# Selective-scan layers: one sequence per scan tile on four row groups of the array, and the product with C moved from VectorE to TensorE

## The reference, cut to what matters

```python
for i in range(4):                                  # N_LAYERS; D_INNER = 256, D_STATE = 16, D_CONV = 4
    u, z = split(x @ in_w[i]); u = silu(causal_conv(u, cw[i]) + cb[i])
    dt, Bm, Cm = split(u @ xpw[i])                  # 8, 16, 16 columns
    delta = softplus(dt @ dtw[i] + dtb[i])
    h[t] = exp(delta[t] * A) * h[t-1] + (delta[t] * u[t]) * Bm[t]     # h: 256 x 16 per sequence
    y[t] = sum over the 16 states n of h[t][:, n] * Cm[t][n]
    x = layer_norm((y + u * D[i]) * silu(z) @ ow[i] + x)
```

## Time and profile before

| | |
|---|---|
| median of 3 runs | 651.4 us |
| the profiled execution | 650.93 us, span 649.0 us |
| PE busy / PEld / DVE / ACT / POOL, share of the span | 85% / 65% / 72% / 48% / 26% |
| first scan of the first unit | 448.75 us |
| end of the last unit's normalisation | 630.27 us |
| TensorE clock granted, mean over the span | 0.758 of 2.4 GHz |

### The profile page before, as it was taken

One profiled execution on the slowest core, in us unless ns is written; L12 is line 12 of the kernel. 1 busy time (PEld: TensorE's weight loads), 2 busy tenths in 40 slices (PEclk: granted clock), 3 DMA queues, 4 the chain that ended last, 5 costly groups with the idle time before them and its releaser, 6 DMA issues.

```text
span 649.0 us, 20759 instructions
## 1 busy us (share of the span) xinstructions
PE 551.3 (85%) x8477; PEld 423.9 (65%) x8477; DVE 467.8 (72%) x1825; ACT 308.3 (48%) x912; POOL 168.7 (26%) x213
## 2 busy tenths in 40 slices
PE   6979877679976999999999999976898889889747
PEld 4646644468865888888888888853664666566335
DVE  2878749964446777777777777724888998899872
ACT  2778657255545443443444443434554554455401
POOL 4255725064000000000000000007437634743600
PEclk9979979899996555555555555555998998899876
DMA  8900000010011000000000000000000000000000
GB/s 317 421 17 1 3 5 1 2 47 1 1 65 36 4 4 4 5 4 5 4 4 5 4 5 4 5 1 1 1 0 2 1 1 2 0 1 2 0 0 10
DMA packets 6304, 16.07 MB, mean 25 GB/s; under 512 B 2680, under 2 KB 3488, under 8 KB 5696
## 3 DMA queue, kind: packets, MB, share of 16 engines
q1 hardware_dynamic: 5792, 14.47, 6.1%
q10 hardware_dynamic: 416, 0.26, 0.1%
HBM read 14.60 MB, written 0.13 MB: 23 GB/s over the span
## 4 chain that ended last, share of the span: by engine, by line
PE 45%; DVE 30%; ACT 13%; issue 8%; POOL 2%; DMA 1%; DVEq 0%; ACTq 0%
PE bank L1728 8%; PE bank L1634 6%; PE bank L1796 6%; ACT esp L684 3%; PE bank L1577 3%; DVE ssum L1172 2%; PE bank L1432 2%; ACT a L671 2%; ACT e L686 2%; PE bank L1422 2%; PE bank L1564 2%; DVE rz L1207 2%; DVE opre L1148 2%; DVE asp L1162 2%; DVE opre L1151 2%
## 5 line engine op out<-in xcount | busy, mean ns | idle before, releaser
L1634 PE MATMUL bank<-esp,qblk 128*128 128x1 f16 (+1 forms) x2048 | 66.6, 166 | 12.0 <-ACT esp L684 12.0
L1634 PEld LDWEIGHTS bank<-esp,qblk 128*128 128x128 f16 x2048 | 61.2, 104 | 17.3 <-ACT esp L684 17.3
L1634 PE MATMUL bank<-hsp,kT 128*128 128x2 f16 x2048 | 63.5, 166 | 2.0 <-DVE hsp L1200 1.9
L1634 PEld LDWEIGHTS bank<-hsp,kT 128*128 128x128 f16 x2048 | 59.5, 104 | 2.1 <-issue 2.1
L475 POOL MEMSET ctxT<- 128x128 f32 x1 | 0.3, 314 | 229.7 <-DVE xres L1214 229.7
L671 ACT ACTIVATE a<-opre 128x4 f32<-128x4 f32 x64 | 13.1, 205 | 80.8 <-DVE opre L1151 80.8
L1240 DVE SCALAR_TENSOR_TENSOR T<-bank,bct,T 128x256 f32<-128x256 f32 x112 | 46.4, 473 | 2.2 <-PE bank L1809 2.2
L1227 DVE TENSOR_TENSOR_SCAN qblk<-ctxT,bank 128x512 f32<-128x512 f32 x32 | 37.7, 1207 | 5.7 <-PE bank L1796 5.3
L678 ACT ACTIVATE gact<-bank,lgate 128x16 f32<-128x16 f32 x64 | 17.5, 274 | 45.7 <-PE bank L1634 45.7
L1227 DVE TENSOR_TENSOR_SCAN w<-kT,bank 128x512 f32<-128x512 f32 x32 | 37.6, 1205 | 1.1 <-PE bank L1796 1.1
L1634 PEld LDWEIGHTS bank<-asp,lsp 128*128 128x128 f16 x768 | 25.5, 105 | 17.1 <-DVE asp L1162 16.8
(11 more groups left out here) (326 smaller groups left out, 1394.8 us busy)
## 6 DMA issues: line engine op xcount, KB each, us to landing
w<-in_w_dram SPq DMA_DIRECT2D x2, 2048.0 KB
ctxT<-in_ctxT_dram SPq DMA_DIRECT2D x8, 256.0 KB, 6.5
wqkv<-in_qkvT_dram SPq DMA_DIRECT2D x1, 1536.0 KB, 11.8
w<-in_mw_dram SPq DMA_DIRECT2D x1, 1024.0 KB, 5.2
lw<-in_lw_dram SPq DMA_DIRECT2D x1, 960.0 KB, 23.1
rows<-in_rows_dram SPq DMA_DIRECT2D x1, 772.0 KB, 8.9
wqkv<-in_fw_dram SPq DMA_DIRECT2D x1, 532.0 KB, 3.5
T<-in_mask_dram SPq DMA_DIRECT2D x1, 512.0 KB, 6.5
```

The source lines that it names most:

```text
L1634: return pe.matmul(out, lhsT, rhs, start=start, stop=stop, skip_group_check=True)
```

## The change

Five things change, all in the state-space layers.

1. *Tiles.* Tile `i` is now channel block `i // 4` and sequence `i % 4`, with all 16 states of that sequence's 32 tokens. Its scan input needs only that sequence's 32 tokens: `scan_input` issues four matmuls with 32 rows, each on its own row group of the array and into its own bank, for one channel block at a time. `diagb` shrinks from 2048 to 512 columns, one POOL instruction in place of four.
2. *Product with C.* A tile is turned as 4 blocks of 128 columns (4 states x 32 tokens), which land on the partitions. ACT copies the turned tiles 0, 2, 4 and 6 and DVE tiles 1, 3, 5 and 7 from PSUM to SBUF (`turned_state`, 128 x 512). PE then multiplies them with a matrix `diagcc` that holds C on diagonals of 32 (`sum_y`, per channel block 16 matmuls of 128 rows, 32 columns of weights and 128 columns that stream, each sequence on its own column group). `read_out` is gone. `diagcc` costs a small POOL product (`m_bcm`, 64 columns), four small matmuls (`turn_c`) and a DVE product of 512 columns (`spread_c`).
3. *Output with tokens on the partitions.* `y` is therefore gated in that layout, turned by PE (`turn_y`), copied by ACT (`turned_y`), and projected.
4. *End of a unit.* `sum_y`, `gate`, `turn_y`, `project_out`, `residual` and `statistics` stand at the end of their own unit, and `centred` and `normalised` ahead of the next unit's first scan, on which `turned(c)` waits.
5. *Banks.* The turned states use bank 7 (tiles 0 to 3, one after another) and banks 0 to 3. The preparation and the residual move to banks 4 to 7, and `m_inv` and `m_a1` to PSUM.

The constants grow by 20 columns. Nothing else of the network is changed.

```diff
-        NT = MN // NG * MC
+        NT = MC * BT
+        CK = MN // NG
-        diagb = [maskb[:, :].bitcast(F32), w1[:, 2048:4096]]
-        cacc = [slot(10, 0), slot(10, 1)]
+        diagb = [T[:, 8 + i, :] for i in range(2)]
+        diagcc = [ws[:, i * 512:(i + 1) * 512] for i in range(2)]
+        hT = [maskb[:, :].bitcast(F32), w1[:, 2048:4096]]
@@ POOL
-                for ng in range(MN // NG):
-                    pool.tensor_tensor(diagb[s][:, ng * 512:(ng + 1) * 512].rearrange("p (n t) -> p n t", t=P),
...
+                pool.tensor_tensor(diagb[s].rearrange("p (n t) -> p n t", t=S), pat(m32, [[0, MN], [1, S]]),
+                                   pat(bct[:, s, 0:MN], [[1, MN], [0, S]]), ALU.mult).then_inc(sem["m_dg"], 1)
+                if c:
+                    pool.wait_ge(sem["m_cs"], c)
+                pool.tensor_tensor(m_bcm.rearrange("p (n b k) -> p n b k", n=NG, b=BT),
...
@@ ACT
+            def turned_state(q, i):
+                if q:
+                    act.wait_ge(sem["m_y"], q)
+                act.wait_ge(sem["turned"], TURNED + q * NT + i + 1)
+                act.activation(hT[i // BT][:, i % BT * 512:(i % BT + 1) * 512], state_bank(i)[:, :], ACT.Copy) \
+                   .then_inc(sem["turned_act"], 1)
@@ DVE
-            def read_out(q, first, end):
-                for n in range(first, end):
...
-                        ins = dve.scalar_tensor_tensor(out=cacc[n % 2], in0=hT, scalar=c_n, in1=cacc[n % 2],
-                                                       op0=ALU.mult, op1=ALU.add)
+            def turned_state(q, i):
...
+                dve.tensor_copy(hT[i // BT][:, i % BT * 512:(i % BT + 1) * 512], state_bank(i)[:, :]) \
+                   .then_inc(sem["turned_dve"], 1)
+            def spread_c(c):
+                dve.wait_ge(sem["m_cs"], c + 1)
+                dve.tensor_tensor(diagcc[c % 2].rearrange("p (n t) -> p n t", t=S),
+                                  pat(bank[4][:, 0:1], [[1, MN], [0, S]], TOK + 2 * MN),
+                                  pat(m32, [[0, MN], [1, S]]), ALU.mult).then_inc(sem["m_prod"], 1)
@@ PE
-                    pe.matmul(bank[i % 4][:, :], duT[s][:, ch * P:(ch + 1) * P], diagb[s][:, ng * 512:(ng + 1) * 512],
-                              start=True, stop=True).then_inc(sem["m_dbu"], 1)
+                for b in range(BT):
+                    own = slice(b * S, (b + 1) * S)
+                    pe.matmul(bank[b][:, :], duT[s][own, ch * P:(ch + 1) * P], diagb[s][own, :], start=True, stop=True) \
+                      .then_inc(sem["m_dbu"], 1)
+            def sum_y(q, ch):
+                pe.wait_ge(sem["turned_act"], TURNED_ACT + q * BT + 2 * (ch + 1))
+                pe.wait_ge(sem["turned_dve"], TURNED_DVE + q * BT + 2 * (ch + 1))
+                for k in range(CK):
+                    for b in range(BT):
+                        at = (b * CK + k) * S
+                        ins = mm(bank[4][b * S:(b + 1) * S, ch * P:(ch + 1) * P], diagcc[q % 2][:, at:at + S],
+                                 hT[ch][:, b * 512 + k * P:b * 512 + (k + 1) * P], stop=(k == CK - 1))
```

More of the change, by code:

```diff
@@ L1300, in _ @@
             gated_z(0)
+            spread_c(0)
             ratio(0)
             first_factor(0)
+            second_factor(0)
             steps_of_time(0)
+            times_u(0)
             for q in range(2 * ML):
                 c = q + 1 if q + 1 < 2 * ML else None
-                scan(q, 0)
                 if q:
-                    gate(q - 1)
-                scan(q, 1)
-                if q:
-                    residual(q - 1)
-                scan(q, 2)
-                if q:
+                    centred(q - 1)
                     normalised(q - 1)
-                for i in range(3, 7):
+                for i in range(0, 4):
                     scan(q, i)
-                read_out(q, 0, 2)
+                turned_state(q, 1)
                 if c:
                     gated_u(c)
-                read_out(q, 2, 3)
+                for i in range(4, 7):
+                    scan(q, i)
+                if c:
+                    gated_z(c)
                 scan(q, 7)
                 if c:
-                    gated_z(c)
-                read_out(q, 3, 6)
-                if c:
                     ratio(c)
-                read_out(q, 6, 8)
+                    spread_c(c)
+                turned_state(q, 3)
+                turned_state(q, 5)
+                turned_state(q, 7)
                 if c:
                     first_factor(c)
+                    second_factor(c)
                     steps_of_time(c)
-                read_out(q, 8, MN)
-            gate(2 * ML - 1)
-            residual(2 * ML - 1)
+                gate(q)
+                if c:
+                    times_u(c)
+                residual(q)
+                statistics(q)
+            centred(2 * ML - 1)
             normalised(2 * ML - 1)
@@ L1432, in x_transpose @@
                     ins = pe.transpose(bank[2 + i % 2][:, c * P:(c + 1) * P], x_soft(i)[:, c * P:(c + 1) * P], ident)
[L1433 removed]
+                ins.then_inc(sem["turned"], 1)
             def x_pv(b):
@@ L1828, in project_out, with turn_y @@
+            def turn_y(q):
+                pe.wait_ge(sem["m_g"], q + 1)
+                for ch in range(MC):
+                    ins = pe.transpose(bank[7][:, ch * P:(ch + 1) * P], m_yt[:, ch * P:(ch + 1) * P], ident)
+                ins.then_inc(sem["m_yT"], 1)
             def project_out(c):
                 l, s = divmod(c, 2)
-                pe.wait_ge(sem["m_g"], c + 1)
+                pe.wait_ge(sem["m_yc"], c + 1)
                 for ch in range(MC):
                     at = (l * MC + ch) * D
-                    ins = mm(bank[5][:, 0:D], m_ys[:, ch * P:(ch + 1) * P], m_out[:, at:at + D],
+                    ins = mm(bank[7][:, 2 * D:3 * D], m_ys[:, ch * P:(ch + 1) * P], m_out[:, at:at + D],
```

340 lines of the change are left out of this document (202 added, 138 removed).

## The result

The changed kernel takes 625.45 us (median of 4 runs, 624.68 to 626.39) against 650.94 us (4 runs, 650.4 to 651.7) before it: ratio 0.961, 95% interval 0.959 to 0.963. Run again beside the experiments it took 624.53 us (5 runs, 624.22 to 624.63) against 650.15, ratio 0.961 (0.960 to 0.963). The forecast was 629 in 620 to 650. The profiled execution took 624.93 us, its span is 623.1 us.

The account below looks back on a forecast made before the run. The prediction took VectorE to bound the unit. Seven steps -22.5 us, last unit -3.4, start +1.8 and hand-overs +2.0 made -22.1: span 649.0 to 628.8 for the profiled execution's 650.93, forecast 629 us, range 620 to 650.

Parts of the forecast that it names:

- The unit at the high clock: One whole state-space unit at full clock: 21.76 us, less 3.4 of DVE work, plus 0.2 of waits, gives 18.55 us.
- the allowance: At a unit's end: four more hand-overs that could not be priced, 0.25 us per unit, +2.0 us together.
- the three places named: DVE's waits in a unit: before `residual` 1.1 us, before `gated_u` 0.4, before `normalised` 0.3.
- all other DVE steps stay: DVE in a unit: apart from read-outs, copies and `spread_c`, its steps keep their times; DVE's work changes by -3.4 us.
- The clock's falls: In the seven steps between first scans: drops of TensorE's clock cost 5.8 us before and were kept at 5.8.
- the last unit's -3.4: The last unit, 23.36 us before, was to lose the same 3.4 us as the others.
- Rival 3: In the units: the clock falls once or twice per unit, costing 1.4 us each, 640 us; chance 0.13.
- rival 1: In the units: the clock is low for most of a unit and PE bounds it, 666 us; chance 0.14.
- VectorE bounds it: In a whole unit: DVE, busy for 20.17 of 21.76 us, sets the pace; its idle time is short waits.
- The start: In the first unit: `ratio` stands behind `spread_c`, uncovered and at the low clock, +1.8 us (+0.5 to +3).
- rival 2: On PE: each of eight shape changes per unit waits for the array to empty, 1.6 us per unit, 642 us; chance 0.05.
- 4: On PE: row and column groups don't run side by side, a unit takes about 27 us, 690 us; chance 0.04.

Follow-up runs that it names:

- thin sum: The changed kernel with `sum_y` for one k of its four, 8 records in place of 32 in each half: 642.05 us, ratio 0.986 to the kernel before.
- the run with full rows: The changed kernel with each scan input as a matmul over all 128 rows instead of one row group: 655.85 us, ratio 1.009 to the kernel before.
- `du` late: The changed kernel with POOL's decay tiles waiting for `du` instead of `delta`: 626.29 us, ratio 0.967 to the kernel before.
- `du` first: The changed kernel with DVE's `times_u` ahead of the gate: 623.22 us, ratio 0.960 to the kernel before.
- `rstd` early: The changed kernel with POOL's decay tiles held until `du` and `rstd` ahead of ACT's second decay exponential: 620.07 us, ratio 0.955 to the kernel before.

## Why the prediction was right, point by point

- **The unit at the high clock: 18.55 forecast, 18.8 with the allowance, 19.02 measured.** DVE's work was to be 20.17 - 3.4 = 16.8 us and is 17.2; the difference is `times_u`, 1.08 for 0.65 us. Copies 0.68 for 0.61 to 0.69, `spread_c` 0.68: as taken. The waits come to 1.8 us (19.01 - 17.21) as forecast, 0.98, 0.21 and 0.20 of them in the three places named, each under its price (1.1, 0.4 and 0.3), and the rest in gaps of 0.1 us or so. For the residual that is two misses that cancel: the chain from the gate's end lasts 1.98 us, not 1.6, since the late `du` stands ahead of the projection, and `times_u` covers 1.0 of it, not 0.6 (by the prediction's own terms 1.6 - 0.6 is 1.0, not 1.1). The step mis-sized is "all other DVE steps stay": POOL's first decay tile was seen to start at `delta`, but not what it does to the one DVE product beside it that reads SBUF alone. Taking the collision away gave nothing until ACT's order was mended too, 0.26 us then: most of the 0.67 us lay beside the projection.
- **The clock's falls: 5.8 us kept, about 1.5 us measured** in the seven steps, all in the first unit (20.57 us at 0.88). I kept them as they were for want of a reason either way. (The unit of 21.76 us, against which they were counted, held some 2 us of low clock itself.) The thin sum shows one reason: `sum_y`'s 64 records stand where the old unit ran out of PE work. The last unit, which prepares no other, has less PE work, and there the clock does fall, for 10.2 us:

```profile
582.29:585.70 3.41, 1.17 (x8) 0.84 (x8) 3.41 (x4) 2.19 (x5) 3.41 (x5) 1.00 0.00 0
585.70:589.11 3.41, 2.20 (x11) 0.58 (x10) 1.86 (x3) 0.86 (x2) 0.80 (x1) 0.50 0.00 0
```

It takes 19.67 us; at a granted 1.00 the run with full rows did its last unit in 17.94, with more PE work in it. That the last unit's -3.4 came out (-3.7) is therefore luck: it would be -5.4 or more at the full clock.

Rival 3 (one or two falls per unit) and rival 1 (most of a unit) did not occur here, but falls in every unit came one edit away from the changed kernel, at 642 us, and low clock for two thirds of a unit one or two edits away from the kernel before, at 694 to 698. Their chance of 0.27 was not too high.
- **"VectorE bounds it": wrong.** With 3.3 us less on DVE the old unit gave 0.3. A busy share of 20.17 in 21.76 does not show a bound when PE has 19.2 in the same 21.76 and the two wait for each other at many places. The sum came out because the change took 3 us from both. PE's saving, which the prediction counted as mere relief, is what the change can't do without (655.85 us). It can't do without VectorE's either: a unit of 19.02 us has no room for 20.2 us of DVE work, though no run took that relief back alone. And the changed order of a unit's end was in every run of the changed kernel; what it is worth by itself is not shown.
- **The start: +1.8 forecast, -1.0 measured.** The new path through `spread_c` costs what was said: from the end of the copy of B and C (438.34) to `ratio` (440.84) it takes 2.5 us where it took 0.87 (440.96 to 441.83). But the copy ended 2.6 us sooner. Of these 0.3 were there before the layers began (the last step of the LSTM's output on ACT starts at 424.82 instead of 425.16); for the rest two causes stand side by side that no run separates: the two matmuls of the convolution's bias, 1.22 us before, run ahead of the chain now (427.13), and the granted clock was high from 435.5 to 438.9, where before it was low until after the first scan. I had priced what was added and not what was moved.
- **The end: 0 forecast, +2.2 measured**, the same instructions at a lower clock. Counted from the last normalisation's start it is 21.4 us here and 19.1 before; it is 21.35 in the second run of the changed kernel and 18.9 in the three runs that only edit an order or a wait (`du` late, `du` first, `rstd` early): it hangs on where the clock stands, not on the change.
- **The sum.** Against the forecast span of 626.9 us: start -2.8, falls -4.3, units +0.22 x 7 = +1.5 beyond the allowance, last unit and its allowance -0.5, end +2.2, which gives 623.0; measured 623.1. The forecast's nearness is in part luck between terms of both signs, of up to 4.3 us.
- **Rivals 2 and 4.** No wait at changes of shape: PE runs scan inputs and bias with starts that overlap the neighbours' ends (bias from 523.56 for 0.48 us, scan inputs from 523.66, bias from 523.88; the ends are the profile's model), which leaves no room for the 0.2 us per change of rival 2. Row and column groups run side by side, 8 records in 1.14 us and 32 in 1.08. The row before that spoke against both the earlier trace rows was a good guide.

## What to carry to other kernels

When two engines are each busy for nine tenths of a stretch, neither is "the bound": price the change as if either were, and take the smaller gain. Where the granted clock falls now and then, look at how much PE work stands in the stretch ahead of each fall, and ask whether the change fills or empties that place; a change that only makes PE's work lighter there can cost more than it saves (17.5 us in the thin sum). The same amount of work can go either way, so try it. When a VectorE operation on SBUF alone comes to stand beside a GpSimd one, look at which of the two starts first, and follow the chain behind it before counting the loss.

## What the runs showed of the hardware

- The low clock lasts though PE is busy: 15.25 us without a gap at 0.50 in the kernel with 32-row scan inputs alone, against 3.4 us in the units of the kernel before, whose scan inputs have 128 rows. But the rows are not all of it. Behind the layers of the changed kernel, where it has the same instructions as the kernel before, PE was busy without a gap for 13.6 us at 0.50:

```profile
606.10:609.50 3.40, 3.40 (x13) 3.04 (x14) 1.99 (x16) 0.22 (x1) 0.00 (x0) 0.50 0.00 0
609.50:619.70 10.20, 10.20 (x29) 6.49 (x28) 0.83 (x4) 1.89 (x4) 0.00 (x0) 0.50 0.00 0
```

In the kernel before, one stretch of 3.4 us over the same instructions (638.80 to 642.20) was granted 0.99. What ends the low clock the runs don't settle.
- Transposes alone can stand ahead of the rise. In the kernel with 32-row scan inputs alone PE ran only transposes from 557.4, at 1.2 GHz, and the clock rose to 2.4 GHz at about 560.8, while they still ran (560.40 to 560.70 at 0.50, 561.00 to 561.30 at 1.00):

```profile
557.41 4.48 PE L1810 MATMUL bank<-cst,w 128*128 128x128 f32 x24
```

The last unit of the changed kernel is nearly the same:

```profile
591.00 4.50 PE L1919 MATMUL bank<-cst,w 128*128 128x128 f32 x20 [0.84 <-ACT maskb L790]
595.29 0.92 PE L1807 MATMUL bank<-projT,T 128*128 128x128 f32 x4
596.15 1.08 PE L1807 MATMUL bank<-maskb,ws 128*32 128x128 f32 x32
```

From 591.0 to 595.3 PE ran nothing but transposes, at 1.2 GHz, then the skip product for 0.6 us, and the stretch from 595.9 was granted 0.99. The Trainium skill (TensorE: Matmul & The Clock Gate, Part 4: PE-mode transpose) says that transposes don't engage the high clock; these rows don't agree.
- A matmul over 32 rows by itself is no shorter than one over 128 (1.12 against 1.02 us for 512 columns); four on four row groups take 1.14 us together.
- A VectorE product of two SBUF tiles of 128 x 256 takes 0.41 us alone, up to 1.13 where a GpSimd tile began just ahead of it (1.08 in the changed kernel, 1.13 in the thin sum), and 0.42 where it began 0.04 us ahead of the GpSimd tile.
